# Null logits in SBUF, an earlier exp and a copy moved to GpSimd in a cross-attention pipeline

## The chip, the cores and the metric

One core of a Trainium2 chip runs the whole program. The metric is the device time of one execution in microseconds; the median of three runs is compared.

## The reference

A stack of four blocks on 128 sequences of 64 tokens with 128 channels, all fp32. Each block is a gated cross-attention to a context of 64 rows with 96 channels, and a gated feed-forward part. The change touches the cross-attentions of blocks 0, 1 and 3, which share one function. Block 3 has a null key and value, one more column for the softmax of every head:

```python
x = x + jnp.tanh(g_xattn[0]) * _L0_xattn_ref(_layernorm(x), ctx_768, mask, ...)
# _L3_xattn_ref
x = layer_norm(x, g_norm)
q = x @ Wq; k, v = jnp.split(context @ Wkv, 2, axis=-1)          # 16 heads of 64
k = jnp.concatenate([nk, k], axis=2)                             # null key first
v = jnp.concatenate([nv, v], axis=2)
sim = jnp.einsum('bhid,bhjd->bhij', q * sqrt_scale, k * sqrt_scale)
sim = jnp.where(full_mask[:, None, None, :], sim, max_neg)
attn = jax.nn.softmax(sim, axis=-1)
out = jnp.einsum('bhij,bhjd->bhid', attn, v).transpose(...).reshape(b, -1, INNER)
return layer_norm(out @ Wout, g_out)
```

Blocks 0 and 1 have 8 heads of 64 and no null key; block 0 is masked, block 1 is not.

## The kernel before

The rows of x are 64 tiles of 128 rows (two sequences each), which stay in SBUF, in 16 groups of four tiles. `wide_attention` is written as one program for each engine. They meet only in semaphores, and each engine's order is fixed by its own text.

A unit is four tiles with 8 heads. In blocks 0 and 1 (below the masked and the unmasked layer) a unit is a group, with 16 units. In block 3 (the null layer) a group takes two passes of 8 heads, so 32 units. The body of each engine's loop covers two units, u = 0 and u = 1, so eight tiles; in the null layer these are the two passes of one group, and the loop has 16 iterations. The step of tile n (t = 0 to 3 in its unit) does the following.

- PE (`step`) transposes the probabilities of tile n into PSUM bank 4 (L746), projects tile n-1 (`project`, L682), multiplies the probabilities with the values (`attend`, L672), computes the scores of tile n+2 (L660, banks 2 and 3), and then the value product of tile n+1 and a key and a query product for a coming unit. These products are three matmuls each on high and low parts (L348 to L350). At t = 1 it also transposes the normalised rows of a coming unit (`turn`, L620); in the null layer it then computes the logits of the null key (`null_scores`, L629).
- ACT evicts the transposed probabilities (L853), takes the exp of tile n+1 (`probs`, L821), evicts a query product (`take_query`, L800), the attention output (L866), the turned rows (`take_hT`, L809), the values (`take_values`, L804) and a key product (`take_key`, L796). `rows_high` (L813) makes the high part of the turned rows, and `take_null` (L817) evicts the null logits to `s0`. ACT works through this list in order.
- DVE does row sums and reciprocal of tile n+1 (`sums`, L922 and L924), then `shift` for tile n+2: scale and mask in PSUM (L904, not in the unmasked layer), maximum (L908), in the null layer the maximum with the null logit (L913) and the null logit less the maximum (L915), and the subtraction (L916). Around it stand the moments (L296, L301) and the scaling (L310) of the layer norms. At t = 0 of the first two layers `add` (L930) and the moments come before `shift`. In the null layer the final norm (`finish_moments`, L941, and `finish_scale`, L947) follows `shift` at t = 1 and t = 2 of the first pass.
- POOL (GpSimd) scales the probabilities of tile n+1 with the reciprocals (`scale_probs`, L549). By the tile it then splits a context chunk into high and low parts (`split`, L524 and L526, t = 0), computes `pow` for the norms (L320; L555 in `finish`), subtracts the high part of the turned rows (`split_rows`, L531), and spreads context parts (`spread`, L539 and L540, t = 3).

PE waits at t = 2 for `hq_low` before the query product, and the transposes of every tile wait for `p_ready` of `scale_probs`. The scores of tile n+2 wait until `shift` of tile n+1 is done. In the null layer `s0` is a corner of PSUM bank 3 that the scores leave free.

Of the kernel before, what the change touches and what calls it, by code (L numbers as in the profile page):

```python
# [8 lines left out]
ALU = mybir.AluOpType  # L9
ACT = mybir.ActivationFunctionType  # L10
AX = mybir.AxisListType

P = 128
S = 64
D = 128
# [377 lines left out]
def wide_attention(c, d, layer):  # L393
# [37 lines left out]
        mask = c.mask  # L431
        nm = [w([TG, S]), w([TG, S])]
    if null:
        r0, r0T, y = w([TG, 2 * HP]), w([GT]), w([TG, D])
        s0 = c.ps[:, 3, S:P].rearrange("p (t h) -> p t h", h=2 * HP)
        fst, fmv, frstd = w([TG, 6]), w([TG, 2]), w([TG])

    jobs = [c.ps[:, 0, :], c.ps[:, 1, :]]
# [46 lines left out]
    def turns(u, t, last):  # L485

        return t == 1 and not last and (u == 0 or not null)
# [7 lines left out]
    with nc.Block() as block:  # L495
# [23 lines left out]
        @block.gpsimd  # L519
        def _(pool):  # L520
            def split(un, raw=cs):
                if raw is cs:
                    pool.wait_ge(cs_in, (un.k - 1) * 16)
                G.tensor_tensor(ch[un.u][0:DC, :], raw[0:DC, :], c.zero[0:DC, 0:GT], ALU.add).then_inc(high, 1)  # L524
                pool.wait_ge(high, un.k + 1)
                G.tensor_tensor(cl[un.u][0:DC, :], raw[0:DC, :], ch[un.u][0:DC, :].bitcast(FP), ALU.subtract).then_inc(low, 1)  # L526

            def split_rows(g, i):

                pool.wait_ge(hq_high, g + 1)  # L530
                G.tensor_tensor(hl[i], hT, hh[i].bitcast(FP), ALU.subtract).then_inc(hq_low, 1)  # L531

            def spread(un, part):

                pool.wait_ge((high, low)[part], un.k + 1)
                src, dst = ((ch, vh), (cl, vl))[part]
                st = src[un.u][0:DC, :].bitcast(FP).rearrange("c (t b k) -> c t b k", b=2, k=S)
                zero = c.zero[0:DC, :].rearrange("c (t b k) -> c t b k", b=2, k=S)
                G.tensor_tensor(dst[un.u][0:DC, :, 0:2, :], st, zero, ALU.add)  # L539
                G.tensor_tensor(dst[un.u][0:DC, :, 2, :], st[:, :, 0, :], zero[:, :, 0, :], ALU.add).then_inc(spread_ready, 1)  # L540

            def scale_probs(n, un, t):

                pool.wait_ge(rec_ready, n + 1)
                if null:
                    if t == 0 and un.p == 0:
                        need(pool, r_ready, un.g)
                    G.tensor_tensor(r0[:, t, un.p * HP:(un.p + 1) * HP], pr[t % 2][:, :, S], rec[t % 2], ALU.mult).then_inc(r0_ready, 1)
                G.tensor_tensor(pn[t % 2], pr[t % 2][:, :, 0:S], bc(rec[t % 2], 2, S), ALU.mult).then_inc(p_ready, 1)  # L549

            def finish(g):
                pool.wait_ge(fin_mv, g + 1)
                G.tensor_tensor(frstd, fmv[:, :, 1], c.w["eps"][:, 0:TG], ALU.add).then_inc(fin_eps, 1)
                pool.wait_ge(fin_eps, g + 1)
                G.tensor_tensor(frstd, frstd, c.w["half"][:, 0:TG], ALU.pow).then_inc(fin_rstd, 1)  # L555

            def add(g):
                xg = norm.xg(g)
                pool.wait_ge(fin_y, g + 1)
                G.tensor_tensor(y, y, bc(c.w["rows"][:, 5, :], 1, TG), ALU.mult).then_inc(fin_yg, 1)  # L560
                pool.wait_ge(fin_yg, g + 1)
                G.tensor_tensor(xg, xg, y, ALU.add).then_inc(added, 1)

            for r in range(norm.n):
                norm.rstd(pool, 0, r)
            pool.wait_ge(low, 1)
            split(second, c.ctx01[:, 0 if null else 1, :])
            spread(first, 0)
            split_rows(0, 0)
            spread(first, 1)  # L570
            for r in range(norm.n):
                norm.rstd(pool, 1, r)
            if not null:
                split_rows(1, 1)
            spread(second, 0), spread(second, 1)
            scale_probs(0, first, 0)
            if not null:
                norm.bias(pool, 0), norm.bias(pool, 1)

            def body(it, last):  # L580
                for u in range(2):
                    for t in range(TG):
                        un, n = Unit(it, u, passes), it * 8 + (4 * u + t)
                        end = last and u == 1
                        if t == 2 and u == 0 and null and not last:
                            split_rows(un.g + 1, 0)
                        if not (end and t == TG - 1):
                            scale_probs(n + 1, *one_on(un, t))
                        if t == 1 and not null and not last:
                            split_rows(un.k + 2, u)  # L590
                        if t == 0 and not last:
                            pool.wait_ge(k_done, un.k * 4 + 4)
                            split(un.next().next())
                        if t == 3 and not last:
                            pool.wait_ge(v_full, n + 1)
                            spread(un.next().next(), 0), spread(un.next().next(), 1)
                        if null:
                            prior = not (isinstance(it, int) and it == 0)
                            if prior and u == 0 and t == 1:
                                finish(it - 1)  # L600
                            if prior and u == 0 and t == 2:
                                add(it - 1)
                            if u == 1 and t < 2 and not (isinstance(it, int) and it >= c.ngroup - 2):
                                norm.rstd(pool, it + 2, t)
                        elif not last:
                            if t == 0:
                                norm.rstd(pool, un.k + 2)
                            if t == 2:
                                norm.bias(pool, un.k + 2)

            by_twos_and_last(pool, units // 2, body)
            if null:
                finish(c.ngroup - 1), add(c.ngroup - 1)
# [179 lines left out]
        def _(act):  # L793
# [12 lines left out]
            def take_hT(g):  # L806
                act.wait_ge(ht_full, g + 1)
                need(act, hq_low, g)
                A.activation(hT, c.ps[:, 4, :], ACT.Copy).then_inc(ht_out, 1)  # L809

            def rows_high(g, i):
                act.wait_ge(ht_out, g + 1)
                A.activation(hh[i], hT, ACT.Copy).then_inc(hq_high, 1)  # L813

            def take_null(g):
                act.wait_ge(z_ready, g + 1)
                A.activation(s0.rearrange("p t h -> p (t h)"), c.ps[:, 2, 0:TG * 2 * HP], ACT.Copy, scale=scale).then_inc(s0_ready, 1)  # L817
# [13 lines left out]
            weights_high(wvh, wv, DC)  # L831
            for j in range(NJ):
                take_key(first, j, j % 2)
            take_hT(0), rows_high(0, 0)
            for j in range(2):
                take_key(second, j, j)
            for j in range(NJ):
# [2 lines left out]
                take_null(0)  # L840
            take_values(0, 0, 0)
            if not null:
                take_hT(1), rows_high(1, 1)
            probs(0, 0)
            take_query(second, 0, 1), take_query(second, 1, 0)

            def body(it, last):
                for u in range(2):
                    for t in range(TG):
# [1 line left out]
                        end = last and u == 1  # L851
                        act.wait_ge(pt_ready, n + 1)
                        A.activation(ptT.rearrange("p j q -> p (j q)"), c.ps[:, 4, :], ACT.Copy).then_inc(pt_out, 1)  # L853
                        if not (end and t == TG - 1) and t != 2:
                            probs(n + 1, t + 1)
                        if had_target(it, u, t, last):
                            take_query(*((target_of(un, t - 1) if t else
                                          (Unit(it, 0, passes).next().next(), 1) if u else (Unit(it - 1, 1, passes).next().next(), 1))),
# [1 line left out]
                        if null and t == TG - 1 and u == 1:  # L860
                            act.wait_ge(r_ready, un.g + 1)
                            A.activation(r0T[0:2 * HP, :], c.ps[0:2 * HP, 4, :], ACT.Copy).then_inc(r0t_ready, 1)
                        if not (end and t == TG - 1) and t == 2:
                            probs(n + 1, t + 1)
                        act.wait_ge(o_ready, n + 1)
                        A.activation(oT.rearrange("p j b q -> p b j q"), ps_o, ACT.Copy).then_inc(ot_out, 1)  # L866
                        if turns(u, t, last):
                            take_hT(un.g + 1 if null else un.k + 2)
                        if not (end and t == TG - 1):
                            take_values(n + 1, t + 1, t % 2)  # L870
                        if turns(u, t, last) and not null:
                            rows_high(un.k + 2, u)
                        if has_target(u, t, last):
                            take_key(*target_of(un, t), 1 - t % 2)
                        if null and t == 0 and u == 0 and not (isinstance(it, int) and it == 0):
                            act.wait_ge(acc_ready, un.g)
                            need(act, added, un.g - 1)
                            A.activation(y.rearrange("p t c -> p (t c)"), c.ps[:, 7, :], ACT.Copy).then_inc(acc_out, 1)
                        if null_turns(u, t, last):
                            take_null(un.g + 1)  # L880
                        if turns(u, t, last) and null:
                            act.wait_ge(q_full, un.k * 4 + 8)
                            rows_high(un.g + 1, 0)

            by_twos(act, units // 2, body)
            if null:
# [1701 lines left out]
```

## Time and profile before

| | us |
|---|---|
| three runs | 3320.51, 3321.71, 3325.45 |
| median | 3321.71 |
| the profiled execution, time | 3320.51 |
| its span, first to last instruction | 3318.7 |
| busy: PE / weight loads / DVE / ACT / POOL | 3017.1 / 2297.6 / 2213.2 / 1545.6 / 1209.0 |
| L549, POOL, 256 times | 267.0, mean 1.043 |
| L922, DVE, 256 times: busy, and idle before it for ACT's L821 | 176.3, and 360.7 |

PE is busy for 91% of the span. Busy time on PE is modelled, because matmuls overlap, so the waits and the distances of starts are more telling than the share. The granted clock is 0.97 of full speed on average and 1.00 within the stretches below. The masked layer lies at about 60 to 420 us of the span, the unmasked one at 1065 to 1430, the null layer at 2480 to 3225.

### The profile page before, as it was taken

The page shows a single profiled execution, that of the slowest core. Times are in us where ns is not written, and L with a number is a line of the kernel's source. Part 1 is how long each engine was busy: PE and PEld are TensorE (multiplying, and loading weights), DVE is VectorE, ACT ScalarE, POOL GpSimd, SP SyncE. Part 2 cuts the span into 40 slices and gives each one's busy share as a digit, 9 for nine tenths or more (in the row PEclk, how much of TensorE's full clock was granted, in tenths as well). Part 3 has the DMA queues.
Part 4 walks back from the last instruction along what each step waited for, and adds up shares of the span by engine and source line. Part 5 has one row for each costly group of instructions (what it writes and reads, how often), then busy time and mean ns, then how long its engine had stood idle before and what let it go on. Part 6 is the DMA issues. An engine that isn't in the chain of part 4 may idle for free. (4 is left out here: it accounts for less than half of the span.)

```text
span 3318.7 us, 90963 instructions
## 1 busy us (share of the span) xinstructions
PE 3017.1 (91%) x35250; PEld 2297.6 (69%) x35250; DVE 2213.2 (67%) x6060; ACT 1545.6 (47%) x2876; POOL 1209.0 (36%) x1408
## 2 busy tenths in 40 slices
PE   3999979999997999969997999999988999999978
PEld 2777735554555777746676888888877777777864
DVE  2666646656664555567876777777767777777755
ACT  1666611211112666626665333333335666666646
POOL 2666510000001666564441000000005666666643
PEclk9999989999998999989998999999999999999989
DMA  5000045665562000011111333333320000000001
GB/s 154 12 9 9 4 129 160 188 184 169 159 192 69 12 8 9 5 46 22 23 27 36 110 102 103 101 103 103 103 80 9 11 7 9 9 7 9 9 1 51
DMA packets 109622, 212.01 MB, mean 64 GB/s; under 512 B 18736, under 2 KB 28912, under 8 KB 108944
## 3 DMA queue, kind: packets, MB, share of 16 engines
q1 hardware_dynamic: 105232, 200.32, 20.7%
q10 hardware_dynamic: 4224, 9.59, 1.0%
q8 instruction: 90, 1.47, 0.2%
q14 instruction: 76, 0.62, 0.1%
HBM read 198.31 MB, written 5.77 MB: 61 GB/s over the span
## 5 line engine op out<-in xcount | busy, mean ns | idle before, releaser
L348 PE MATMUL ps<-parts 128*128 128x512 f32 (+2 forms) x1568 | 640.9, 409 | 46.5 <-DVE parts L954 27.6
L349 PE MATMUL ps<-parts 128*128 128x512 f32 (+2 forms) x1568 | 566.0, 361 | 0.0
L350 PE MATMUL ps<-parts 128*128 128x512 f32 (+2 forms) x1568 | 563.1, 359 | 0.0
L318 POOL TENSOR_TENSOR rstd<-mv,eps 128x4 f32<-128x4 f32 x112 | 24.0, 214 | 1222.1 <-DVE mv L301 1222.1
L348 PEld LDWEIGHTS ps<-parts 128*128 128x128 f32 (+1 forms) x1568 | 299.3, 191 | 185.2 <-ACT work L804 100.0
L922 DVE TENSOR_REDUCE work<-work 128x8 f32<-128x512 f32 (+1 forms) x256 | 176.3, 689 | 360.7 <-ACT work L821 360.7
L1853 ACT ACTIVATE work<-ps 128x512 f32<-128x512 f32 x272 | 163.0, 599 | 452.6 <-PE ps L350 452.4
L549 POOL TENSOR_TENSOR work<-work 128x512 f32<-128x512 f32 x256 | 267.0, 1043 | 231.3 <-DVE work L924 229.0
L350 PEld LDWEIGHTS ps<-parts 128*128 128x128 f32 (+1 forms) x1568 | 299.1, 191 | 45.9
L349 PEld LDWEIGHTS ps<-parts 128*128 128x128 f32 (+1 forms) x1568 | 301.2, 192 | 13.6
L1819 PEld LDWEIGHTS ps<-early,work 128*128 128x128 f32 x2176 | 281.6, 191 | 29.8 <-DVE work L1910 11.4
L1819 PE MATMUL ps<-early,work 128*128 128x128 f32 x2176 | 289.4, 276 | 8.1 <-DVE x L2017 8.1
L1900 DVE TENSOR_TENSOR work<-work,ps 128x512 f32<-128x512 f32 x272 | 185.9, 683 | 133.5 <-PE ps L1819 123.7
L2171 PE MATMUL ps<-work,early 128*128 128x512 f32 x512 | 249.5, 610 | 11.5 <-DVE work L2392 11.5
L853 ACT ACTIVATE work<-ps 128x512 f32<-128x512 f32 x256 | 152.6, 596 | 199.9 <-PE ps L746 199.9
L804 ACT ACTIVATE work<-ps 128x512 f32<-128x512 f32 x256 | 153.0, 597 | 174.2 <-PE ps L350 171.2
L746 PE MATMUL ps<-ident,work 128*128 128x128 f32 x1024 | 157.3, 276 | 38.3 <-POOL work L549 38.3
L1910 DVE TENSOR_TENSOR work<-work 128x512 f32<-128x512 f32 x256 | 177.2, 692 | 15.4 <-DMA work<-expert_rows 2.8
L908 DVE TENSOR_REDUCE work<-ps 128x8 f32<-128x512 f32 x256 | 176.2, 688 | 9.6 <-PE ps L660 2.7
L672 PE MATMUL ps<-work 64*64 64x64 f32 x8192 | 179.6, 226 | 2.3 <-ACT work L853 2.3
L2392 DVE TENSOR_TENSOR work<-work 128x1024 f32<-128x1024 f32 x128 | 154.6, 1219 | 38.7 <-DMA work<-gate_rows 35.7
L916 DVE TENSOR_TENSOR work<-ps,work 128x512 f32<-128x512 f32 x256 | 175.6, 686 | 4.4
(311 smaller groups left out, 6162.8 us busy)
## 6 DMA issues: line engine op xcount, KB each, us to landing
work<-gate_rows SPq DMA_DIRECT2D x128, 512.0 KB, 5.5
work<-expert_rows SPq DMA_DIRECT2D x512, 128.0 KB, 2.9
work<-gate_rows SPq DMA_DIRECT2D x128, 256.0 KB, 7.7
work<-in_ctxT SPq DMA_DIRECT2D x72, 192.0 KB, 2.4
out<-x SPq DMA_DIRECT2D x16, 256.0 KB, 2.3
work<-work SPq DMA_DIRECT2D x224, 16.0 KB
work<-work SPq DMA_DIRECT2D x16, 128.0 KB, 2.9
early<-in_l0f_w ACTq DMA_DIRECT2D x1, 1536.0 KB, 12.1
```

Source lines behind the costliest of these rows:

```text
L348: T.matmul(out, lh, rh, start=True, stop=False)
L349: T.matmul(out, lh, rl, start=False, stop=False)
L350: return T.matmul(out, ll, rh, start=False, stop=True)
L549: G.tensor_tensor(pn[t % 2], pr[t % 2][:, :, 0:S], bc(rec[t % 2], 2, S), ALU.mult).then_inc(p_ready, 1)
L672: last = T.matmul(ps_o[e * DH:e * DH + DH, b, j, :], vp[t % 2][rows, e, j, :], ptT[rows, j, b * S:b * S + S], start=True, stop=True)
L908: V.tensor_reduce(mx[t % 2], ps_s, AX.X, ALU.max).then_inc(max_ready, 1)
L916: V.tensor_tensor(banks(sc[t % 2][:, :, 0:S]), ps_s.rearrange("p (s j) k -> p s j k", s=2), bc(tops, 3, S), ALU.subtract).then_inc(sub_rea ...
L922: V.tensor_reduce(den[t % 2], pr[t % 2], AX.X, ALU.add).then_inc(sum_ready, 1)
L1819: last = T.matmul(acc[:, t * D:(t + 1) * D], aT[b][:, t * P:(t + 1) * P], c.w["l2f_d"][:, j, :], start=(j == 0 and t == 0), stop=(j == NB ...
L1900: out = V.tensor_tensor(aT[b], sg[b], ps_u[b], ALU.mult)
L1910: V.tensor_tensor(aT[b], aT[b], wb[j % WR], ALU.mult).then_inc(a_ready, 1)
L2171: T.matmul(ps_q[u], c.w["l0f_w"][:, at:at + P], hw[p % NHW][:, e, :], start=(p == 0 and e == 0), stop=(p == NP - 1 and e == 1))
```

## The change

Three edits, all in `wide_attention`.

1. `s0`, the null logits, gets its own place in SBUF.
2. The high part of the turned rows is made by POOL, as an addition of zero at the head of `split_rows`, and no longer by ACT (`rows_high` goes). In the null layer POOL takes over the wait on `q_full` ahead of it, at t = 2 of the first pass.
3. ACT takes the exp of tile n+2 at the end of step n, and no longer that of tile n+1 in the middle of step n. One more `probs` stands ahead of the loop.

```diff
     if null:
-        r0, r0T, y = w([TG, 2 * HP]), w([GT]), w([TG, D])
-        s0 = c.ps[:, 3, S:P].rearrange("p (t h) -> p t h", h=2 * HP)
+        s0, r0, r0T, y = w([TG, 2 * HP]), w([TG, 2 * HP]), w([GT]), w([TG, D])
...
             def split_rows(g, i):
 
+                pool.wait_ge(ht_out, g + 1)
+                G.tensor_tensor(hh[i], hT, c.zero[:, 0:GT], ALU.add).then_inc(hq_high, 1)
                 pool.wait_ge(hq_high, g + 1)
                 G.tensor_tensor(hl[i], hT, hh[i].bitcast(FP), ALU.subtract).then_inc(hq_low, 1)
...
                         if t == 2 and u == 0 and null and not last:
+                            pool.wait_ge(q_full, un.k * 4 + 8)
                             split_rows(un.g + 1, 0)
...
-            def rows_high(g, i):
-                act.wait_ge(ht_out, g + 1)
-                A.activation(hh[i], hT, ACT.Copy).then_inc(hq_high, 1)
...
-            take_hT(0), rows_high(0, 0)
+            take_hT(0)
...
             if not null:
-                take_hT(1), rows_high(1, 1)
+                take_hT(1)
             probs(0, 0)
             take_query(second, 0, 1), take_query(second, 1, 0)
+            probs(1, 1)
...
                         A.activation(ptT.rearrange("p j q -> p (j q)"), c.ps[:, 4, :], ACT.Copy).then_inc(pt_out, 1)
-                        if not (end and t == TG - 1) and t != 2:
-                            probs(n + 1, t + 1)
...
-                        if not (end and t == TG - 1) and t == 2:
-                            probs(n + 1, t + 1)
                         act.wait_ge(o_ready, n + 1)
...
-                        if turns(u, t, last) and not null:
-                            rows_high(un.k + 2, u)
...
+                        if t < 2 or not end:
+                            probs(n + 2, t)
                         if null_turns(u, t, last):
                             take_null(un.g + 1)
-                        if turns(u, t, last) and null:
-                            act.wait_ge(q_full, un.k * 4 + 8)
-                            rows_high(un.g + 1, 0)
```

## Rows read from the trace of the kernel before

**Rows 1.** PE's waits, 80 to 430 us and 1060 to 1440 us: engine, waited for, us in total, times, longest.
```profile
PE ps L620 <- DVE work L310: 17.6, 13, 1.4
...
PE ps L620 <- DVE work L310: 18.1, 13, 1.4
```

**Rows 2.** Windows, busy us of each engine: one null-layer iteration, one masked-layer unit.
```profile
2801.85:2846.13 44.28, 43.15 (x744) 35.25 (x744) 32.65 (x97) 29.06 (x53) 29.73 (x38) 1.00 0.03 9
200.38:222.21 21.83, 20.53 (x357) 17.11 (x356) 14.89 (x36) 14.44 (x27) 14.28 (x15) 1.00 0.03 9
```

**Rows 3.** Timeline of PE, masked layer: start, us, line, form, count, idle before.
```profile
211.85 0.60 PE L746 MATMUL ps<-ident,work 128*128 128x128 f32 x4
212.28 1.06 PE L682 MATMUL ps<-early,work 128*128 128x128 f32 x8
...
213.78 0.65 PE L660 MATMUL ps<-work 64*64 64x64 f32 x32
...
216.82 0.60 PE L746 MATMUL ps<-ident,work 128*128 128x128 f32 x4
...
218.24 0.69 PE L672 MATMUL ps<-work 64*64 64x64 f32 x32
...
220.80 0.66 PE L620 MATMUL ps<-ident,work 128*128 128x128 f32 x4 [1.30 <-DVE work L310]
```

**Rows 4.** Timeline of DVE, same stretch.
```profile
213.63 0.69 DVE L922 TENSOR_REDUCE work<-work 128x8 f32<-128x512 f32 x1 [1.95 <-ACT work L821]
...
214.67 0.75 DVE L930 SCALAR_TENSOR_TENSOR x<-ps,tg,x 128x512 f32 x1
...
217.97 0.69 DVE L916 TENSOR_TENSOR work<-ps,work 128x512 f32<-128x512 f32 x1
219.63 1.12 DVE L310 TENSOR_SCALAR work<-x,mv,rstd 128x128 f32 x4 [0.97 <-POOL rstd L320]
```

**Rows 5.** Timeline of POOL, same stretch.
```profile
210.64 1.28 POOL L539 TENSOR_TENSOR parts<-parts,zero 96x512 fp32r<-96x512 f32 x1
...
214.63 1.04 POOL L549 TENSOR_TENSOR work<-work 128x512 f32<-128x512 f32 x1
215.64 1.28 POOL L524 TENSOR_TENSOR parts<-work,zero 96x512 fp32r<-96x512 f32 x1
...
218.50 1.02 POOL L320 TENSOR_TENSOR rstd<-rstd,half 128x4 f32<-128x4 f32 x1
```

**Rows 6.** Timeline of ACT, same stretch.
```profile
212.48 0.60 ACT L853 ACTIVATE work<-ps 128x512 f32<-128x512 f32 x1 [0.80 <-PE ps L746]
212.98 0.62 ACT L821 ACTIVATE work<-work 128x512 f32<-128x512 f32 x1
```

**Rows 7.** Timeline of DVE, null layer.
```profile
2820.92 0.70 DVE L904 SCALAR_TENSOR_TENSOR ps<-ps,work 128x512 f32<-128x512 f32 x1 [0.20 <-PE ps L660]
...
2822.38 0.16 DVE L913 TENSOR_TENSOR work<-work,ps 128x8 f32<-128x8 f32 x1
...
2822.66 0.68 DVE L916 TENSOR_TENSOR work<-ps,work 128x512 f32<-128x512 f32 x1
```

**Rows 8.** Timeline of POOL, null layer, first pass, third tile.
```profile
2835.99 1.01 POOL L555 TENSOR_TENSOR work<-work,half 128x4 f32<-128x4 f32 x1
2836.98 1.28 POOL L531 TENSOR_TENSOR parts<-work,parts 128x512 fp32r<-128x512 f32 x1
```

**Rows 9.** Timeline of PE, null layer, first pass, third and fourth tile.
```profile
2839.17 0.50 PE L348 MATMUL ps<-parts 128*128 128x512 f32 x1
...
2846.13 0.65 PE L746 MATMUL ps<-ident,work 128*128 128x128 f32 x4 [1.02 <-POOL work L549]
```

**Rows 10.** Two lines of DVE over the whole trace: duration ns min/median/max, first and last start.
```profile
L915 DVE TENSOR_TENSOR work<-ps,work x128: 171/172/176, 2504.4 to 3208.8; 128x8 f32<-128x8 f32 x128
...
L954 DVE TENSOR_TENSOR parts<-early,parts x6: 653/676/677, 56.3 to 1062.1; 96x512 fp32r<-96x512 f32 x4, 128x512 fp32r<-128x512 f32 x2
...
L954 DVE TENSOR_TENSOR parts<-l_wv,parts x2: 1578/1678/1777, 2496.2 to 2497.7; 96x512 fp32r<-96x512 f32 x2
```

## Prediction

> **What bounds the kernel now.** I read the waits of PE first. In the two layers without a null key, the masked one and the unmasked one, PE has one kind of repeated stall: the turning transposes of `turn` (L620) wait for the normalised rows that DVE writes (L310), 13 times in each layer, 17.6 and 18.1 us in all, so 1.35 and 1.39 us a time [rows 1]. Then the windows: of a 21.83 us unit in the masked layer PE is busy 20.5 us, and of a 44.28 us iteration (eight tiles) of the null layer 43.2 us [rows 2]. So PE sets the pace in both, and an edit pays only where PE waits, or costs only where it makes PE wait.
>
> Then the timelines, to see what the wait hangs on. Of the masked layer the reader is to see a step as PE has it: transposes of the probabilities at T (211.85), the projection ending at T+1.49, scores ending at T+2.58 (214.43), the next transposes at T+4.97, and `attend` (L672) 1.42 after the transposes [rows 3]. The turn starts at 220.80, when L310 ends at 220.75, although PE could have turned 1.3 us earlier. L310 waited for POOL's `pow` (L320), which ended at 219.52, and POOL got there late because it worked without a break from 210.64: spreads to 214.55, `scale_probs` (L549), split, rstd [rows 4, 5]. The front of that queue was set by DVE's row sums (L922), which waited 1.95 us for ACT's exp (L821), and exp sat behind the eviction of the tile before (L853) [rows 4, 6].
>
> **The change part by part.**
>
> *exp moved (`probs(n + 2)` at the end of step n).* The exp of the next tile is now done before ACT waits for PE's transposes. Sums and reciprocal then come at about T+0.5 to T+1.4 in place of T+1.8 to T+2.7 (213.63 to 214.5) [rows 4]. POOL starts its fourth-tile `scale_probs`, and so the spreads behind it, 1.3 us earlier. Its work from there to L320 is gapless, so rstd comes at 218.2 in place of 219.52, and L310 ends near 219.45: about when the scores of that step end. The turn stall goes: 13 times 1.35 and 13 times 1.39, **-17.6 and -18.1 us**.
>
> What is late next: ACT is in order, so the probabilities' eviction now waits for exp, which waits for DVE's shift of tile n+2. Its chain is: scores end, 0.07, shift, 0.06, exp, 0.5 to the start of the eviction (the distance of two ACT starts), 0.6, 0.06, attend and scores 1.16 (213.27 to 214.43) [rows 3, 6]. The null layer's shift takes 2.42 us from L904 to the end of L916, of which the two small operations are 0.3 [rows 7]; so the masked layer's takes 2.1, and the ring closes in 4.6 us, under 4.97. But in each unit's first tile DVE puts `add` and the moments before the shift. `add` can't start before the projection's end, 213.34, so it starts 1.28 earlier than 214.67 and the shift ends at 217.38 in place of 218.66 [rows 3, 4]. exp is then 217.44, the eviction starts at 217.97 and ends at 218.57: attend at 218.63 in place of 218.24, **+0.4 us for each of 13 units, +5.2 us**. In the unmasked layer the shift is 0.73 shorter (no L904), so nothing is left.
>
> *The high part moved from ACT to POOL.* ACT's copy takes about 0.62 us, POOL's about 1.28, the duration of its subtraction of the same shape (L531) [rows 6, 8]. In the steady units of the two first layers it comes after `ht_out` while POOL is idle, and the low part is then ready near T+1.2 of the third tile, where the query job reads it at T+4.2: no cost; without that cover it would be 0.65 each. At the start of the layers it is serial, twice in two layers and once in the third: 5 x 0.65, **+3.2 us**.
> In the null layer it is not covered. POOL's `finish` (L555) ends at 2837.00; the low part now ends at 2839.6 in place of 2838.26, and the query job is due at 2839.17 [rows 8, 9]. `scale_probs` of the fourth tile, behind it, moves by 1.3 too, so that tile's transposes come 0.85 later. A tile on, POOL's `add` and `scale_probs` cost PE 1.02 now [rows 9]; they hang on `finish_scale`, which follows the third tile's shift and comes 1.1 earlier, as DVE's sums no longer hold that shift up. The two cancel within 0.3. The new wait on `q_full` heads POOL's third tile: split, `scale_probs` and `add` queue behind it, but those queries ended before the tile began. Nothing. Alone, moves of exp and high part give the null layer -0.1 us an iteration, bounds -1 and +1.
>
> *s0 from PSUM to SBUF.* This is the dear part. L913 and L915 of `shift` read one operand from PSUM and one from SBUF, and L915 takes 171 to 176 ns in all 128 cases, though POOL is busy for 29.7 of 44.3 us [rows 2, 7, 10]. After the change both have two SBUF operands. The trace has DVE subtractions of that kind (L954): 653 to 677 ns with POOL quiet, but 1578 and 1777 ns in the two cases where POOL was in the middle of its spreads: each waited for the POOL instruction to end [rows 10]. That POOL's next instruction then slips in ahead of a DVE one that follows a semaphore is what I read from it.
> The Trainium skill (SBUF — State Buffer, Who interferes with whom) says that a DVE instruction with two SBUF inputs and a GpSimd one that reads SBUF exclude each other for a whole instruction, and that one with a single SBUF input doesn't contend. The rows have it only for 512 columns; by the rule it holds for 8 too, and the sum is then the one below, without it that of the first rival.
>
> The price, bounded: nothing if 8 columns don't contend; at most two whole POOL instructions, 2.56 us, a shift. I go by where POOL is. In the null layer the ring closes in 4.9 us, and a plain step is about 5.0, so some 0.1 us is free [rows 3, 7]. L913 comes 2.7 us after attend. `scale_probs` of the tile starts 0.45 after attend and lasts 1.2.
> - Second pass, first tile: spreads and `scale_probs` to 1.95, then the split's 1.28 and 1.28 [rows 5]. L913 waits to 3.2, L915 for the second half to 4.6: 1.6 late, 1.5 on PE.
> - First pass, first tile: same without the spreads, 1.3 late, 1.2 on PE.
> - First pass, third tile: PE waits for the query rows and `scale_probs` behind L913's and L915's turns: 1.3 more than now.
> - First pass, fourth tile: POOL's `add`, `scale_probs`, spreads: 1.7 late, but 1.2 of stall is there already: 0.4 more.
> - Second pass, third tile: moments, sums and mask rows delay the shift: 0.3.
> - Second pass, fourth tile: 0.75 late under the 16-row transposes and projections. Nothing. The second tiles find POOL idle.
>
> Together 4.7, less 0.1 for the other moves: 4.6 us an iteration, 15 iterations, **+69 us**.
> The Trainium skill (Perfetto Trace Analysis, Optimizing Scalar/DVE Operations) puts DVE's access cost at some 60 ns on SBUF and 125 on PSUM. By that the move would shorten each shift by 0.13 us, and the sum would be lower by at most some 4 us. No row has it at this shape.
>
> Sum: 3318.7 - 17.6 - 18.1 + 5.2 + 3.2 + 69 = **3360.4 us** of span. The profiled execution took 1.8 us more than its span (3320.51) and 1.2 less than the median, 3321.71. So 3362; the last units of each layer, with short steps, I put at -1: **3361 us**, 1.2% slower.
>
> **The rivals.**
> 1. *No contention at 8 columns.* The null layer is then worth -1.5, the sum 3318.7 - 27.3 - 1.5 - 1 + 1.8: **3291, faster by 0.9%**. For it: all rows of contention are of wide operands. Against: the two L954 waited for POOL's end, which has nothing to do with their width. It decides at the null iteration's price of 1.8 us (27.3/15): below that the change is faster.
> 2. *One wait a shift, not two.* L913 waits, and L915 follows it before POOL starts anew. First tiles then lose 0.5 and 0, the fourth 0, the third 1: about 1.2 an iteration, +18: **3310**, faster by 0.3%. For it: a gap of 40 ns between the two. Against: POOL's next instruction is queued already.
> 3. *Worse phase.* Second tiles are hit too, POOL itself is pushed back by DVE: two more waits of 1.1 an iteration, +33: **3394**.
> 4. *The turn stall stays*, since POOL doesn't get ahead: +30.5 on the forecast, **3391**. Against: POOL's gapless run from 210.64.
>
> **How the numbers follow.** Forecast 0.66 (own range 3330 to 3385), rival 1 0.14, rival 2 0.09, rivals 3 and 4 0.11 together. From the forecast down to 3300 and up to 3390 leaves out rival 1 and half of the last two: the range is **3300 to 3390**. 0.2% (6.6 us) is about what a measurement can tell here. Faster: rival 1, most of 2, 0.21; same, the edge of 2 and a null iteration priced at 2 us: 0.05; slower 0.74.
>
> **What the changed profile would show.** L620 waiting for L310 hardly at all in the first two layers; exp (L821) straight after the key eviction; L922 no longer waiting for it. In the null layer L913 and L915 with medians still near 0.17 us but a maximum over 1 us, mean near 0.5, and an iteration of about 48.9 us in place of 44.28; PE waiting for ACT's eviction before L672. If L913 and L915 stay at 0.2 us, the forecast is wrong in sign.

## The result and the profile after

The changed kernel takes **3341.45 us** (median of four runs, 3339.3 to 3343.11); the kernel before takes 3321.68 in the same comparison. The ratio is **1.0057, 95% interval 1.0040 to 1.0075**: slower by 19.8 us. The forecast was slower by 39.3. The sign held and the time lies in the range; the size was twice what came.

The profiled execution of the changed kernel has a span of 3332.9 us and a time of 3334.95, which is 6.5 under its median; the one of the kernel before is 1.2 under its own. So sums from the trace (+14.2 us of span) stand some 5 us under the medians' difference.

Line numbers move by one or two, or back by eight or nine: `turn` L620 is L622, `attend` L672 is L674, scores L660 are L662, transposes L746 are L748, exp L821 is L819, the eviction L853 is L852, the maximum with the null logit L913 is L905, the null logit less the maximum L915 is L907. POOL's copy that makes the high part is L530, its subtraction L532.

First PE's waits, which answer to [rows 1]: two rows for 80 to 430 us, then three for the null layer, 2480 to 3240 us. Columns: waited for, us in total, times, longest.

```profile
PE ps L674 <- ACT work L852: 12.7, 18, 1.6
PE ps L2153 <- DVE work L2377: 7.4, 1, 7.4
...
PE ps L674 <- ACT work L852: 47.3, 61, 1.6
PE ps L348 <- POOL parts L532: 9.1, 14, 0.7
PE ps L748 <- POOL work L550: 8.8, 3, 6.8
```

(L2153 belongs to the block behind the masked layer.) In the kernel before, the first row of the null layer, 2480 to 3225 us, was another one:

```profile
PE ps L746 <- POOL work L549: 26.8, 19, 6.9
```

The turn's wait for L310 is gone from the list, in the unmasked layer too. In its place `attend` waits for the eviction of the probabilities: 12.7 us in the masked layer and 47.3 in the null layer, 61 times, four in an iteration. That is the ring of shift, exp and eviction: each waits for the one before it, and `attend` and the next scores for the eviction. In the null layer the transposes' wait for POOL's scaled probabilities, 26.8 us before, is down to 8.8.

The windows that answer to [rows 2]: one about as long as a unit of the masked layer, and one as long as a null iteration.

```profile
208.18:229.00 20.82, 20.32 (x356) 16.88 (x356) 14.65 (x36) 14.16 (x26) 15.27 (x15) 1.00 0.03 9
...
2743.90:2791.20 47.30, 43.39 (x745) 35.39 (x744) 37.28 (x98) 29.33 (x53) 30.93 (x40) 1.00 0.03 8
```

From transposes to transposes a unit takes 20.93 us in the mean of the masked layer's 2nd to 14th unit, in place of 21.88; the iteration went from 44.28 to 47.30. PE is as busy as before (43.39 to 43.15); DVE is busy for 37.28 in place of 32.65, 4.6 us more. The two small operations hold 4.5 of it, as the rows that answer to [rows 10] show (ns min/median/max, first and last start):

```profile
L905 DVE TENSOR_TENSOR work<-work x128: 166/169/928, 2476.7 to 3224.2; 128x8 f32<-128x8 f32 x128
...
L907 DVE TENSOR_TENSOR work<-work x128: 172/174/1872, 2476.9 to 3224.4; 128x8 f32<-128x8 f32 x128
```

The median is as before, the mean 368 and 527 ns against 162 and 172: 60 of the 128 instances of L905 and 45 of L907 take over 250 ns. Grouped by place, the layers' change in the profiled executions (first to last transposes, or last value product) is this:

| stretch | before | after | change | forecast |
|---|---|---|---|---|
| start, to the masked layer's first transposes | 79.78 | 79.01 | -0.8 | part of the starts' +3.2 |
| masked layer | 337.67 | 327.29 | -10.4 | -17.6 + 5.2 |
| unmasked layer | 337.26 | 317.17 | -20.1 | -18.1 |
| from there to the null layer | 1092.46 | 1095.94 | +3.5 | part of the starts' +3.2 |
| null layer | 704.20 | 747.26 | +43.1 | +69 |
| all else | | | -1.1 | -1 |

The stretch ahead of a layer's first transposes holds the layer's own start. There PE's product of the query rows waits for the low part, from POOL, longer than before. The unmasked layer's start, after the change:

```profile
1057.72 0.50 PE L348 MATMUL ps<-parts 128*128 128x512 f32 x1 [2.03 <-POOL parts L532]
...
1067.28 0.79 PE L348 MATMUL ps<-parts 128*128 128x512 f32 x1 [3.42 <-POOL parts L532]
...
1072.22 0.63 PE L748 MATMUL ps<-ident,work 128*128 128x128 f32 x4 [1.30 <-POOL work L550]
```

Before, the two waits were 1.31 and 2.75. From the beginning of the first wait to the first transposes it was 1068.10 to 1083.24, 15.14 us; it is 1055.69 to 1072.22, 16.53. The masked layer's start grew by the same (15.14 to 16.59), the null layer's by 1.9 (24.44 to 26.33, from its first product's start). So the starts cost 1.4 + 1.5 + 1.9 = 4.8 us. That the first row of the table is negative comes of the loads and the stretch ahead of the layer, which were 2.2 us quicker in this execution; over the other kernels they differ by as much.

Now a null iteration, from the last tile of the first pass to the second pass's first two tiles. POOL, start and us:

```profile
2742.86 1.04 POOL L550 TENSOR_TENSOR work<-work 128x512 f32<-128x512 f32 x1
2743.86 1.27 POOL L540 TENSOR_TENSOR parts<-parts,zero 96x512 fp32r<-96x512 f32 x1
...
2748.86 1.28 POOL L523 TENSOR_TENSOR parts<-work,zero 96x512 fp32r<-96x512 f32 x1
2750.22 1.30 POOL L525 TENSOR_TENSOR parts<-work,parts 96x512 fp32r<-96x512 f32 x1
...
2773.14 1.27 POOL L525 TENSOR_TENSOR parts<-work,parts 96x512 fp32r<-96x512 f32 x1
```

DVE in the same stretch:

```profile
2743.26 0.67 DVE L905 TENSOR_TENSOR work<-work 128x8 f32<-128x8 f32 x1
2743.96 1.21 DVE L907 TENSOR_TENSOR work<-work 128x8 f32<-128x8 f32 x1
...
2749.76 0.41 DVE L905 TENSOR_TENSOR work<-work 128x8 f32<-128x8 f32 x1
2750.20 0.17 DVE L907 TENSOR_TENSOR work<-work 128x8 f32<-128x8 f32 x1
...
2773.07 0.17 DVE L905 TENSOR_TENSOR work<-work 128x8 f32<-128x8 f32 x1
2773.27 1.18 DVE L907 TENSOR_TENSOR work<-work 128x8 f32<-128x8 f32 x1
```

And what follows on ACT and PE (the bracket is the idle time before, and what ended it):

```profile
2745.80 0.64 ACT L819 ACTIVATE work<-work 128x520 f32<-128x520 f32 x1 [1.83 <-DVE work L908]
2746.34 0.58 ACT L852 ACTIVATE work<-ps 128x512 f32<-128x512 f32 x1
...
2747.07 0.69 PE L674 MATMUL ps<-work 64*64 64x64 f32 x32 [1.44 <-ACT work L852]
2752.27 0.69 PE L674 MATMUL ps<-work 64*64 64x64 f32 x32 [0.16 <-ACT work L852]
...
2770.20 0.69 PE L674 MATMUL ps<-work 64*64 64x64 f32 x32 [0.45 <-ACT work L852]
2776.34 0.69 PE L674 MATMUL ps<-work 64*64 64x64 f32 x32 [0.97 <-ACT work L852]
```

Three places, three outcomes. At 2743.26 L905 waits till POOL's L550 ends at 2743.90; POOL's next instruction starts at once, and L907 waits for the whole of it, to 2745.17. PE loses 1.44. At 2749.76 L905 waits till L523 ends at 2750.14; the split's second instruction, which has a semaphore to wait for, starts only at 2750.22, and L907 at 2750.20 is through ahead of it. PE loses 0.16. At 2773.07 the same gap falls on L905, which passes free, and L907 is the one that stands behind L525: 1.18, PE loses 0.97. The four stalls of an iteration add up to 1.44 + 0.16 + 0.45 + 0.97 = 3.02 us. That this is also the iteration's growth is chance: PE waits another 0.66 for the low part (L532) at the first pass's third tile, and the 1.02 us that it waited for L549 before is gone.

### The profile page after: what moved, and what is told of

Its sections match the earlier page's. It is cut to its first block and busy times, and to the rows that moved or that the text cites. A ratio compares the mean times of both kernels' runs of the same rounds, so it can differ in the third digit from the quotient of the medians.

```text
span 3332.9 us, 90975 instructions
## 1 busy us (share of the span) xinstructions
PE 3017.0 (91%) x35250; PEld 2298.1 (69%) x35250; DVE 2284.3 (69%) x6060; ACT 1545.4 (46%) x2828; POOL 1267.3 (38%) x1456
## 5 line engine op out<-in xcount | busy, mean ns | idle before, releaser
L550 POOL TENSOR_TENSOR work<-work 128x512 f32<-128x512 f32 x256 | 266.9, 1042 | 183.5 <-DVE work L916 180.4
L896 DVE SCALAR_TENSOR_TENSOR ps<-ps,work 128x512 f32<-128x512 f32 x192 | 133.9, 697 | 155.9 <-PE ps L662 145.6
L674 PE MATMUL ps<-work 64*64 64x64 f32 x8192 | 179.6, 225 | 63.0 <-ACT work L852 63.0
L819 ACT ACTIVATE work<-work 128x512 f32<-128x512 f32 (+1 forms) x256 | 161.9, 632 | 125.4 <-DVE work L908 123.5
L674 PEld LDWEIGHTS ps<-work 64*64 64x64 f32 x8192 | 146.8, 135 | 100.0 <-issue 81.3
## 6 DMA issues: line engine op xcount, KB each, us to landing
early<-in_l0f_w ACTq DMA_DIRECT2D x1, 1536.0 KB, 12.3
```

The source lines that it names most:

```text
L674: last = T.matmul(ps_o[e * DH:e * DH + DH, b, j, :], vp[t % 2][rows, e, j, :], ptT[rows, j, b * S:b * S + S], start=True, stop=True)
```

## The experiments

Theory: the price is that of two small DVE operations which both read only SBUF while POOL is at work, and it reaches PE through exp and the eviction. Rivals: the price comes of the other two edits (exp ahead of the eviction, the high part on POOL), or of having the null logits in SBUF in some other way than through POOL. Each kernel ran beside the kernel before, whose medians were 3323.79 (first four), 3323.18 (next three) and 3321.81 (last).

**All but the SBUF tile (e1_s0_psum).** The changed kernel with `s0` back in PSUM.

```diff
-        s0, r0, r0T, y = w([TG, 2 * HP]), w([TG, 2 * HP]), w([GT]), w([TG, D])
+        r0, r0T, y = w([TG, 2 * HP]), w([GT]), w([TG, D])
+        s0 = c.ps[:, 3, S:P].rearrange("p (t h) -> p t h", h=2 * HP)
```

> The changed kernel with the null logits back in the free corner of the PSUM bank; exp and high part stay moved. Theory (two SBUF operands make the two small DVE operations of the shift wait for GpSimd): both back at 0.16 and 0.17 us in all 128 cases, the null iteration from 47.3 to about 44.2 us, so 15 x 3.1 = 46 us less than the changed kernel's 3341: 3295, range 3285 to 3300, faster than before by 0.8%. Rival (the null layer lost its time to the later high part and the exp that holds up ACT's eviction, and the operands' place does not matter): still 47 us an iteration and 3335 or more.

Measured: 3294.66 us (3291.71 to 3295.84), ratio 0.9911 (0.9896 to 0.9926). The null iteration takes 44.00 us. DVE's small operations, grouped by line (busy us, mean ns, idle before):

```profile
L908 DVE TENSOR_TENSOR work<-ps,work 128x8 f32<-128x8 f32 x128 | 22.0, 172 | 4.4
L906 DVE TENSOR_TENSOR work<-work,ps 128x8 f32<-128x8 f32 x128 | 20.7, 161 | 5.5
```

PE's wait for the eviction in the null layer is 4.9 us, 4 times, in place of 47.3. So moving the null logits, 64 values a row, from one memory to the other costs 3341.45 - 3294.66 = 46.8 us, more than the whole loss, and without it the change would have been a gain.

**The SBUF tile alone (e2_s0_only).** The kernel before with the first line of that diff in place of the second and third.

> The kernel before with the null logits in SBUF and nothing else. Theory: the two small DVE operations contend here too (maxima over 1 us, means 0.3 to 0.5), but in this kernel exp stands a step later, about 1 us behind the shift's end, so a shift that is 1 to 1.6 us late reaches PE only in part: 3322 to 3335, most likely 3327. Rival (the contention costs PE its full amount whatever stands behind it): about 3.1 us an iteration, 3365. Rival (no contention): 3320 to 3322 and maxima of 0.2 us.

Measured: 3347.89 us (3344.64 to 3351.99), ratio 1.0076 (1.0063 to 1.009): a miss, by 13 to 26 us. The small operations wait nearly as much, 404 and 408 ns in the mean. What I had taken for free was the place where the shift's end is due first. PE's timeline, and below it two windows of one tile each (the first also holds the null scores and the stall):

```profile
2818.02 0.64 PE L745 MATMUL ps<-ident,work 128*128 128x128 f32 x4
2824.53 0.75 PE L628 MATMUL ps<-l_wnull,work 128*64 128x16 f32 x16 [1.31 <-DVE work L915]
2825.21 1.12 PE L745 MATMUL ps<-ident,work 128*128 128x128 f32 x4
2826.12 1.92 PE L681 MATMUL ps<-l_wo,work 128*128 128x128 f32 x8
```

```profile
2818.02:2825.21 7.19, 5.88 (x105) 4.74 (x105) 7.01 (x22) 3.40 (x6) 4.83 (x6) 0.98 0.09 27
2825.21:2831.67 6.46, 6.46 (x90) 5.52 (x89) 4.79 (x18) 3.62 (x7) 2.41 (x4) 0.76 0.00 0
```

`null_scores` (L628) waits 1.31 us for the shift (L915 here), since its results go to the bank that this shift still reads. And behind that stall the granted clock is 0.76 over the next tile: the transposes take 1.12 us in place of 0.64, the projection 1.92 in place of 1.06. Iterations take 45.5 us where the clock stays at 1.00, 1.2 to 1.3 more than before, and 47.0 to 47.2 in the 5 of 15 where it falls, about 1.5 more again. 15 x 1.25 + 5 x 1.5 = 26, against 24.1 measured.

**The early exp alone (e3_exp_only).** The kernel before with the `probs` lines of the change and nothing else (`rows_high` stays on ACT, `s0` in PSUM).

> The kernel before with only the exp moved. Theory: the turn stalls go in both layers without a null key (-17.6 -18.1 +5.2), no start cost of the high part (that is 3.2), and in the null layer the 1.02 us wait in each iteration goes without the query rows being late: 15 x -1. About 3275, range 3268 to 3285. Rival (the later high part is what gives the room on ACT, so exp and the high part's copy together on ACT delay the eviction in each turning step): 3290 to 3300, no better than the version with both moved.

Measured: 3278.4 us (3275.95 to 3281.35), ratio 0.9861 (0.9846 to 0.9876), as expected. This is the best version of all: 45.4 us faster than before. The masked layer takes 327.99 us and the unmasked one 319.63, which is the changed kernel's gain but for 2.5 us in the unmasked one (327.29 and 317.17), and the null iteration 43.49, 0.79 less than before.

**The high part alone (e4_high_only).** The kernel before with edit 2 only.

> The kernel before with only the high part moved to GpSimd. Theory: 3 us at the starts of the layers, and in the null layer the fourth tile of the first pass is 0.85 us later but the next one is bound by add and scale_probs as before, so nothing more: 3325, range 3321 to 3330. Rival (the delay on GpSimd adds up through the iteration): 0.85 to 1.3 us x 15, so 3335 to 3344.

Measured: 3323.69 us (3322.35 to 3331.55), ratio 1.0005 (0.9996 to 1.0014): no change. The null iteration is 44.29 us, and inside it the step of the first pass's third tile is 6.10 in place of 5.23 and the next one 5.29 in place of 6.16: a delay and its recovery. The first layer's transposes come 2.0 us later (81.77); the profiled execution, at 3331.55 us, is the longest of the eleven and 7.9 above their median, so its places say more of where than of how much. Next to the early exp the edit isn't free, though: it is all that stands between `e3_exp_only` and `e1_s0_psum`, 3294.66 - 3278.4 = 16.3 us. 0.51 x 15 = 7.7 of them are the iteration (44.00 against 43.49); the three starts, read as above, are longer by 1.3, 2.6 and 0.7, together 4.6. In the unmasked start 1.2 of the 2.6 lie behind the first wait: it lasts 1.98 us, and over the 4 us behind it the granted clock is 0.59, where the changed kernel has 1.00 behind a wait of 2.03. The last 4 are hardly in the traces: the two profiled executions lie 3294.32 - 3281.35 = 13.0 apart and not 16.3, since the one of `e3_exp_only` is the longest of its four, and of those 13.0 the iterations and the starts are 12.3.

**One operation of the two (e5_one_sbuf).** The changed kernel with a second copy of the null logits in PSUM, one more ACT copy in a group, and the maximum reading that one.

```diff
+        s1 = c.ps[:, 3, S:P].rearrange("p (t h) -> p t h", h=2 * HP)
...
+                A.activation(s1.rearrange("p t h -> p (t h)"), c.ps[:, 2, 0:TG * 2 * HP], ACT.Copy, scale=scale)
                 A.activation(s0.rearrange("p t h -> p (t h)"), c.ps[:, 2, 0:TG * 2 * HP], ACT.Copy, scale=scale).then_inc(s0_ready, 1)
...
-                        V.tensor_tensor(tops, tops, banks(s0[:, t, un.p * HP:(un.p + 1) * HP]), ALU.max)
+                        V.tensor_tensor(tops, tops, banks(s1[:, t, un.p * HP:(un.p + 1) * HP]), ALU.max)
```

> The changed kernel, but the null logits are written to both places (a second 0.2 us copy on ACT, 16 times): the maximum reads the PSUM copy, so it has one SBUF operand, and only the subtraction of the null column has two. Theory (each of the two waits for GpSimd on its own, and the second one for a whole instruction more): the maximum is back at 0.16 us in all cases, the subtraction waits only for the rest of what runs, mean about 0.35 to 0.45 us. The late shifts of 1.6 us become 0.6, so PE loses about 1.2 us less in the fourth tile of the first pass, 0.5 in the first and last tiles: 45.3 us an iteration in place of 47.3, about 3312, range 3303 to 3320. Rival (it is one collision a shift, whichever operation has it): 3335 to 3343.

Measured: 3306.62 us (3305.45 to 3308.48), ratio 0.9952 (0.9939 to 0.9966), in the expected range. The iteration takes 44.8 us. The two lines, subtraction and maximum:

```profile
L909 DVE TENSOR_TENSOR work<-work 128x8 f32<-128x8 f32 x128 | 42.6, 333 | 4.4
L907 DVE TENSOR_TENSOR work<-work,ps 128x8 f32<-128x8 f32 x128 | 20.7, 162 | 5.5
```

The one with a PSUM operand is at 162 ns again although it stands at the same place in time and works on the same tile; the one with two SBUF operands still waits. One such operation, with the extra copy, costs 12.0 us against `e1_s0_psum`, two cost 46.8. The waits go nearly in the same measure: over the durations with a PSUM operand, 0.16 us a shift here and 0.56 in the changed kernel. The other half, two SBUF operands in the maximum alone, did not run.

**The change but for the high part (e7_exp_s0).** The early exp and the SBUF tile, `rows_high` on ACT.

> The changed kernel with the high part back on ACT: exp and null logits stay moved. Theory: the price of the SBUF operands is the same as with the high part on GpSimd, 46 us above the version with only exp moved (3278): 3325, range 3318 to 3330. Rival (the high part on GpSimd is what fills it at the moment of the shift): 30 us or less, 3308.

Measured: 3328.66 us (3327.23 to 3329.78), ratio 1.0018 (1.0009 to 1.0027), as expected. Against the early exp alone the tile costs 3328.66 - 3278.4 = 50.3 us, so its price hardly depends on the edit of the high part. The iteration is about 47.0, its small operations take 377 and 526 ns.

**Gaps between POOL's instructions (e6_gaps).** If a gap of 80 ns lets both operations through, more gaps should help. The changed kernel with a wait on POOL's own last instruction ahead of each spread instruction.

```diff
-                G.tensor_tensor(dst[un.u][0:DC, :, 0:2, :], st, zero, ALU.add)
+                G.tensor_tensor(dst[un.u][0:DC, :, 0:2, :], st, zero, ALU.add).then_inc(spread_mid, 1)
+                pool.wait_ge(spread_mid, un.k * 2 + part + 1)
...
+                            pool.wait_ge(p_ready, n + 2)
                             spread(un.next().next(), 0)
+                            pool.wait_ge(spread_ready, un.k * 2 + 5)
                             spread(un.next().next(), 1)
```

> The changed kernel, but GpSimd waits for its own last instruction ahead of each of the spreads' instructions, which leaves gaps of about 80 ns as there is one between the two halves of the split. The work is the same. Theory (DVE gets the port at the end of the running instruction, and where a gap follows, both small operations pass in it): the shifts in the fourth tiles of both passes are about 1 us earlier, PE's wait for ACT's eviction of 1.44 us in the first tile of the second pass falls to below 0.5, the one of 0.45 goes; the collision with the split in the first pass stays. Iteration 46.0 in place of 47.3, about 3321, range 3315 to 3330. Rival (GpSimd and DVE take turns whatever the gap): no change or slightly slower, 3341 to 3346.

Measured: 3337.33 us (3336.77 to 3337.83), ratio 1.0044 (1.003 to 1.0058): 4 us better than the change, 16 short of what I expected. DVE, then PE:

```profile
2750.37 0.67 DVE L909 TENSOR_TENSOR work<-work 128x8 f32<-128x8 f32 x1
2751.07 0.17 DVE L911 TENSOR_TENSOR work<-work 128x8 f32<-128x8 f32 x1
2755.84 0.74 DVE L909 TENSOR_TENSOR work<-work 128x8 f32<-128x8 f32 x1
2756.61 1.21 DVE L911 TENSOR_TENSOR work<-work 128x8 f32<-128x8 f32 x1
...
2753.14 0.69 PE L678 MATMUL ps<-work 64*64 64x64 f32 x32 [0.42 <-ACT work L856]
2759.71 0.69 PE L678 MATMUL ps<-work 64*64 64x64 f32 x32 [1.52 <-ACT work L856]
```

Where the gaps stand they work: ahead of the first spread L911 takes 0.17 in place of 1.21, and PE's stall falls from 1.44 to 0.42. But the next tile now meets POOL's `scale_probs` and split back to back (no gap there), and its stall is 1.52 in place of 0.16. In all the iteration falls from 47.3 to 46.7 us and the null layer by 8. The rest of the gain is lost elsewhere: `spread` serves all three layers, and with its gaps the unmasked layer takes 323.10 us in place of 317.17. There the turn waits for L310 again, 13 times, 5.6 us. So the collisions moved in part, and in part the gaps were paid for where nothing collides.

**Gaps there too (e8_all_gaps).** The same, with a wait between the two operations of `scale_probs` and one ahead of the split.

```diff
+                    pool.wait_ge(r0_ready, n + 1)
...
                             pool.wait_ge(k_done, un.k * 4 + 4)
+                            pool.wait_ge(p_ready, n + 2)
```

> The changed kernel with the gaps of the run before, and also a gap ahead of the split and one between the two operations of scale_probs, so that every instruction of GpSimd that can meet the small operations is followed by a gap. Theory: no subtraction waits for a whole further instruction; its maximum of 1.2 us or more in the stretch falls, the mean of the two together from 0.9 us in the changed kernel to about 0.55. What is left is the rest of one running instruction, as where only one operation has two SBUF operands. PE's stall of 1.52 us in the first pass's side of the ring falls to about 0.4: 45.7 us an iteration, about 3321, range 3313 to 3332. Rival (the collisions only move on to another tile, as they did with the first set of gaps): 46.5 us and more, 3334 to 3341.

Measured: 3354.1 us (3344.09 to 3359.99), ratio 1.0092 (1.0077 to 1.0107): a miss by 33 us. Maximum and subtraction:

```profile
L911 DVE TENSOR_TENSOR work<-work 128x8 f32<-128x8 f32 x128 | 70.2, 549 | 5.5
L913 DVE TENSOR_TENSOR work<-work 128x8 f32<-128x8 f32 x128 | 23.2, 181 | 4.4
```

The mechanism did what it was to do: with a gap behind nearly each POOL instruction the second operation hardly waits any more (181 ns in the mean). The first waits more (549), and the iteration only falls to 47.0. POOL's longer queue brings the turn's wait back: for L310, 13 times in each layer, 3.8 us in the masked and 8.9 in the unmasked one. By layer, the null layer is 3.7 us shorter than in the changed kernel, while the masked and the unmasked one are 6.2 and 10.0 longer and the stretches ahead of the three layers 10.6. Gaps in the null layer alone did not run. Of its runs, the three at 3357 us and more have a mean granted clock of 0.964, the three at 3351 and less 0.969 to 0.971; I didn't follow that up.

The single edits and their combinations (medians, us; the kernel before took 3321.68 to 3323.79 beside them, and the high part with the SBUF tile but the old exp did not run):

| | `s0` in PSUM | `s0` in SBUF |
|---|---|---|
| before | 3321.68 | 3347.89 |
| high part on POOL | 3323.69 | |
| early exp | 3278.4 | 3328.66 |
| both | 3294.66 | 3341.45 |

## Why the prediction was right or wrong

**The turn.** Right in its mechanism. -17.6 and -18.1 with +5.2 for the `add` ahead of the shift make -30.5 for the two layers; they became 10.4 and 20.1 us shorter, 30.5. That the sums agree to a tenth is luck: the masked layer came out 2.0 short of its forecast of -12.4 and the unmasked one 2.0 beyond its -18.1. The 13 steady units hold what was worked out, -12.4 and -17.8. The ends of the layers do the rest, for which the sum has -1 in all: in the last four tiles of the masked layer, with their short steps, the new ring costs PE 1.3 us each. The rows that answer to [rows 3, 4, 5], in the order POOL, DVE, PE:

```profile
212.64 1.02 POOL L320 TENSOR_TENSOR rstd<-rstd,half 128x4 f32<-128x4 f32 x1
...
213.76 1.12 DVE L310 TENSOR_SCALAR work<-x,mv,rstd 128x128 f32 x4 [0.86 <-POOL rstd L320]
...
214.20 0.69 PE L674 MATMUL ps<-work 64*64 64x64 f32 x32 [0.50 <-ACT work L852]
214.68 0.68 PE L662 MATMUL ps<-work 64*64 64x64 f32 x32
215.29 0.65 PE L622 MATMUL ps<-ident,work 128*128 128x128 f32 x4
```

L310 ends at 214.88 while the scores still run, and the turn follows them without a wait. The 0.50 ahead of `attend` is the new ring: 0.4 was forecast, and it is 0.35 to 0.50 in the 13 units.

**The high part.** In the null layer two moves of 1.3 and 1.1 us were to cancel. With the old exp they do (44.29 against 44.28). At the starts +3.2 was forecast and 4.8 came; each of PE's waits there grew by 0.7, as forecast, 1.0 in the null layer, 3.8 together; the last 1.0 lies behind the waits. With the early exp the edit costs 16.3 us. I had worked the two edits out together as -0.1 an iteration; they give -0.28 (44.00), of which the early exp is -0.79 and the high part +0.51.

**The SBUF tile.** The mechanism is the one forecast: two operations of 128x8 that read SBUF alone wait for the POOL instruction in progress, and the second of them for the next as well. The first rival, no contention at 8 columns, is out: L907 took 1.2 us again and again in the steady iterations, and 1.87 once. The Trainium skill (SBUF — State Buffer, Who interferes with whom) states the exclusion without naming a width, and that an operation with one SBUF input is spared. The traces agree on both, 527 ns against 172 in the mean for the same subtraction. The second rival, one wait a shift, is out as the rule, yet holds at one place, and that is the step that failed. The third, hits in the second tiles too, is out: those steps moved by -0.07 us together. So is the fourth, since the turn's stall went.

**The step that failed is in the price of the SBUF tile: "Second pass, first tile: spreads and `scale_probs` to 1.95, then the split's 1.28 and 1.28 [rows 5]. L913 waits to 3.2, L915 for the second half to 4.6: 1.6 late, 1.5 on PE."** L905 (the old L913) did wait for the split's first half to end, but L907 (the old L915) not for the second, which starts only 80 ns after that end. Measured: 5.02 to 5.20 us from `attend` to `attend`, +0.18. That is 1.3 an iteration and 15 x 1.3 = 20 us of the 69. All steps, from `attend` to `attend`:

| step to the next tile | forecast | measured |
|---|---|---|
| second pass, first tile | +1.5 | +0.18 |
| second pass, third | +0.3 | +0.10 |
| second pass, fourth | 0 | +0.52 |
| first pass, first | +1.2 | +1.05 |
| first pass, third | +1.3 | +0.96 |
| first pass, fourth | +0.4 | +0.28 |
| the two second tiles, other moves | -0.1 | -0.07 |
| iteration | +4.6 | +3.02 |

15 x 3.02 = 45.3 in place of 69: 23.7 of the 26.5 us between the forecast span (3360.4 - 1) and the measured 3332.9. Two smaller steps failed as well and cancel in part. The first pass's third tile cost 0.96 in place of 1.3. The second pass's fourth tile, put at nothing because the late shift would lie under the 16-row transposes and projections, cost 0.52: PE waits 0.45 there for the eviction. Where a semaphore stands between two POOL instructions was in the program's text and in the trace of before (the split's two halves start 1.36 apart and last 1.28), and I counted the split as 2.56 us without a break.

**From span to median.** The prediction names two steps, 1.8 us from the span to the time and 1.2 from the profiled execution to the median, and adds only the first. With both it would have ended at 3362 in place of 3361.

**The access cost.** The Trainium skill (Perfetto Trace Analysis, Optimizing Scalar/DVE Operations) would have given back 0.13 us a shift. No run shows it: the shortest L905 and L907 take 166 and 172 ns from SBUF, and with a PSUM operand the same two take 162 and 172 in the mean.

**Shown and argued.** Shown by leaving single edits out or doing them alone: the tile's price (46.8, and 50.3 without the high part), the gain of the early exp (45.4), nothing for the high part alone, and that the SBUF operands are the cause of each operation's wait. That the gap decides which operation waits is shown at single places of the traces and by the mean of the subtraction, 527 ns without added gaps and 181 with them everywhere. That added gaps win time is not shown: both forms that ran missed their forecast, at -4 and +13 us against the change. Both also laid gaps in the layers without null logits, so whether gaps in the null layer alone would pay stays open. Why the clock falls behind some stalls and not behind others stays open too.

## What to carry to other kernels

Before a small DVE operand moves from PSUM to SBUF, look at what its instruction is left with: if all its inputs are then in SBUF and POOL is busy, each such instruction can cost about one POOL instruction, as those of 8 columns did here (up to 1.2 us in the steady iterations), and two in a row more than one. Price it by place: for each instance, which POOL instruction runs, whether a wait stands between it and the next, and how much slack the chain behind has. Expect a mended place to shift the collision to the next tile, and a wait added in shared code to cost something in the layers that had no collision. A change of three edits is best timed as three: here one gave -45, one 0 to +16 and one +24 to +50.

## What the hardware showed that I had not expected

- The gap that a satisfied wait leaves between two POOL instructions, 80 to 90 ns, is enough for one or two DVE operations of 170 ns to get ahead (L907 at 2750.20 against L525 at 2750.22). POOL instructions without one start 30 to 40 ns before the end of the last is recorded, and a DVE operation that comes 60 ns after that end waits for the whole next one (L907 at 2743.96).
- A PE stall of 1.31 us in `e2_s0_only` was followed by 6.46 us at a granted clock of 0.76, at which the transposes took 1.12 us in place of 0.64. The same stall of 1.31 us at the same place of another iteration of the same trace (2593.70) was followed by 6.33 us at 1.00, and stalls of 1.44 us in the changed kernel by nothing of the kind either (1.00 over the whole iteration). What else tells them apart was not tried.
